# A selected LSTM step by step: the output gate multiplied after the choice of the weight set is known

## The reference

```python
x = x + gnn(layernorm(x))              # 10 rounds of graph propagation, 1250 nodes, 512 channels
x = x + lstm(layernorm(x)[None])[0]    # batch 1, 1250 steps, H = 512, S = 4 weight sets

def step(carry, x_t):
    h, c = carry
    sel_in = jnp.concatenate([h, c, x_t], axis=-1)
    logits = sel_in @ W_sel.T + b_sel
    onehot = jax.nn.one_hot(jnp.argmax(logits, axis=-1), Sx, dtype=x_t.dtype)
    g_all = einsum('bi,sgi->bsg', x_t, W_ih) + einsum('bh,sgh->bsg', h, W_hh) + b_ih + b_hh
    g = jnp.einsum('bsg,bs->bg', g_all, onehot)
    h2, c2 = _lstm_activate(g, c)      # i, f, g, o; c2 = s(f) c + s(i) tanh(g); h2 = s(o) tanh(c2)
    return ((h2, c2), h2)
```

## Time and profile before

| | us |
|---|---|
| median of the runs | 7712.02 |
| profiled execution | 7713.46 |
| its span | 7711.7 |
| loop A, 1484 to 2834 | 1350, 256 steps |
| loop B, 2842 to 7690 | 4848, 994 steps |
| PE busy | 6634.8 (86%) |
| DVE busy | 3545.5 (46%) |
| ACT busy | 1004.7 (13%) |

### The profile page before, as it was taken

One profiled execution on the slowest core, in us unless ns is written; L12 is line 12 of the kernel. 1 busy time (PEld: TensorE's weight loads), 2 busy tenths in 40 slices (PEclk: granted clock), 3 DMA queues, 4 the chain that ended last, 5 costly groups with the idle time before them and its releaser, 6 DMA issues. The chain is left out here.

```text
span 7711.7 us, 250693 instructions
## 1 busy us (share of the span) xinstructions
PE 6634.8 (86%) x85214; PEld 3513.4 (46%) x85215; DVE 3545.5 (46%) x16895; ACT 1004.7 (13%) x4031; POOL 945.3 (12%) x2829
## 2 busy tenths in 40 slices
PE   3467998899999998888888888888888888888888
PEld 3433444655555554444444444444444444444444
DVE  5523112355555554444444444444444444444444
ACT  0011001311111111111111111111111111111111
POOL 5703112200000000000000000000000000000000
PEclk6588998999999999999999999999999999999999
DMA  3220001622222210000000000000000000000000
GB/s 83 0 68 0 0 0 40 224 78 81 80 84 77 83 56 8 4 8 4 8 8 4 8 4 8 6 7 8 4 8 7 6 8 4 8 4 8 8 4 24
DMA packets 292938, 220.00 MB, mean 29 GB/s; under 512 B 137196, under 2 KB 268652, under 8 KB 290609
## 3 DMA queue, kind: packets, MB, share of 16 engines
q1 hardware_dynamic: 162612, 160.58, 6.2%
q10 hardware_dynamic: 106110, 59.01, 3.0%
q0 software_dynamic: 24192, 0.10, 1.0%
HBM read 160.28 MB, written 59.36 MB: 28 GB/s over the span
## 5 line engine op out<-in xcount | busy, mean ns | idle before, releaser
L1021 PE MATMUL ps<-WH,hparts 128*17 128x512 f16 x49760 | 2969.1, 380 | 148.9 <-DVE hparts L864 63.7
L1021 PEld LDWEIGHTS ps<-WH,hparts 128*17 128x17 f16 x49760 | 1305.0, 91 | 1316.2 <-DVE hparts L864 242.7
L840 DVE STREAM_TRANSPOSE gateT<-ps 128x512 f32<-128x512 f32 x1250 | 896.0, 717 | 2097.2 <-PE ps L1057 2088.0
L1091 PE MATMUL ps<-WH 128*128 128x512 f16 x4970 | 1246.1, 381 | 0.0
L467 POOL COPY xT<-hfull 128x4 f32 x1250 | 239.9, 192 | 5386.9 <-DVE hparts L862 5386.9
L1008 PE MATMUL ps<-wselT,acts 128*1 128x4 f32 x10000 | 430.5, 166 | 407.1 <-DVE acts L852 407.1
L972 PE MATMUL ps<-O,Adj 128*128 128x512 f16 x3000 | 650.3, 380 | 77.2 <-DVEq L749 77.2
L1091 PEld LDWEIGHTS ps<-WH 128*128 128x128 f16 x4970 | 404.6, 97 | 630.8 <-issue 278.7
L581 ACT ACTIVATE gateT<-gblk 128x16 f32 x1250 | 289.3, 231 | 2660.9 <-DVE pick L835 2618.4
L585 ACT ACTIVATE acts<-gates 128x16 f32<-128x16 f32 x1250 | 269.8, 216 | 2239.8 <-DVE gates L844 2239.8
L1065 PE MATMUL ps<-xT,wih_next 128*128 x2048 | 501.1, 388 | 65.1 <-DMA wih_next<-in_w_ih 34.0
(11 more groups left out here) (141 smaller groups left out, 4547.4 us busy)
## 6 DMA issues: line engine op xcount, KB each, us to landing
wih_next<-in_w_ih SPq DMA_DIRECT2D x256, 256.0 KB, 2.9
gblk<-gate_inputs ACTq DMA_DIRECT2D x48, 800.0 KB, 5.0
gate_inputs<-gx_next SPq DMA_DIRECT2D x64, 500.0 KB, 2.6
wst<-in_w_hh ACTq DMA_DIRECT2D x32, 512.0 KB, 7.6
wih<-in_w_ih SPq DMA_DIRECT2D x16, 1024.0 KB, 8.6
adjacency<-Adj SPq DMA_DIRECT2D x2, 6400.5 KB, 24.7
Adj<-adjacency SPq DMA_DIRECT2D x2, 6400.0 KB, 26.8
gate_inputs<-gstage SPq DMA_DIRECT2D x16, 500.0 KB, 6.0
```

What stands on the lines that cost most here:

```text
L840: dve.transpose(gateT[:, :, 0:32], gate_ps.rearrange("p (c q) -> p c q", q=32)).then_inc(turned, 1)
L1021: nc.tensor.matmul(gate_ps[32 * j:32 * j + 17, :], hparts[:, k, :], WH[:, s * KC + k, part, j, :], start=(k == 0 and part == 0), stop=(k = ...
L1091: nc.tensor.matmul(ps[:, 2, :], WH[:, 0, 0, 0, 0:P], WH[:, 0, 0, 0, :], start=True, stop=True)
```

## The change

Four things change, all in `cell` on DVE, in `act_block` on ACT, and in the step of PE.

1. The product is split. The cell part (input, forget and candidate gates) is multiplied with the guess, the output gate's part only once the pick is known. The input and forget gates take one matmul of 256 columns, the candidate one of 128 columns that goes into the forget gate's columns of PSUM, with the stationary operand shifted by one column, so that its sums land in rows 1 and 17 instead of 0 and 16. `gate_ps` shrinks to 256 columns. The output gate has a bank of its own, `ogate_ps`, 128 columns.
2. The seal goes. DVE now waits for `guess_mm` (four increments, one from the last matmul of each column group) and `settled` (either four at once from the sequencer of PE, when the guess was right, or one from each group's last matmul of the repeated cell part).
3. The output gate has its own chain: a transposing reduction out of PSUM, an addition of the input's share, and a tanh of its own on ACT. `osig` and `owsel` wait for that tanh.
4. PE's sequencer branches on the guess first. All else of a step, the logits too, stands within each of the four branches, and so does the comparison with the pick. The next guess is loaded behind the products and ahead of the pick. The weights of the selector are no longer scaled by 2^-13, and `owsel` is made from the tanh in one operation.

```diff
-                dve.wait_ge(gates_mm, n)
+                dve.wait_ge(guess_mm, n4)
+                dve.wait_ge(settled, n4)
                 dve.transpose(gateT[:, :, 0:32], gate_ps.rearrange("p (c q) -> p c q", q=32)).then_inc(turned, 1)
...
-                dve.tensor_reduce(gates[:, :], gateT[:, :, 0:33:16], AX.X, ALU.add).then_inc(gates_ready, 1)
+                dve.tensor_reduce(gates[:, :].rearrange("p (r b) -> p r b", r=2), turned_terms, AX.X, ALU.add).then_inc(gates_ready, 1)
+
+                dve.wait_ge(ogate_mm, n4)
+                dve.tensor_reduce(osum[:, 0, :], ogate_ps.rearrange("p (c q) -> p c q", q=32), AX.X, ALU.add,
+                                  apply_transpose=True).then_inc(oturned, 1)
+                dve.wait_ge(gates_ready, n)
+                dve.wait_ge(oturned, n)
+                dve.tensor_tensor(osum[:, 1, :], osum[:, 0, :], gates[:, 2 * SUB:3 * SUB], ALU.add).then_inc(osum_ready, 1)
...
-            def logits(t, n):
+            def logits(n):
...
-                pe.wait_ge(c_ready, n)
+                pe.wait_ge(owsel_ready, n)
...
+            def cell_products(s, done):
+
                 for k in range(KC):
                     for part in range(2):
                         for j in range(4):
-                            nc.tensor.matmul(gate_ps[32 * j:32 * j + 17, :], hparts[:, k, :], WH[:, s * KC + k, part, j, :],
-                                             start=(k == 0 and part == 0), stop=(k == KC - 1 and part == 1),
-                                             tile_position=(0, 32 * j))
+                            nc.tensor.matmul(gate_ps[32 * j:32 * j + 18, :], hparts[:, k, 1:19], WH[:, s * KC + k, part, j, 0:2 * P],
+                                             start=(k == 0 and part == 0), stop=False, tile_position=(0, 32 * j))
+                        for j in range(4):
+                            last = nc.tensor.matmul(gate_ps[32 * j:32 * j + 18, P:2 * P], hparts[:, k, 0:18],
+                                                    WH[:, s * KC + k, part, j, 3 * P:4 * P],
+                                                    start=False, stop=(k == KC - 1 and part == 1), tile_position=(0, 32 * j))
+                            if k == KC - 1 and part == 1:
+                                last.then_inc(done, 1)
+
+            def output_products(s):
+                for k in range(KC):
+                    for part in range(2):
+                        for j in range(4):
+                            last = nc.tensor.matmul(ogate_ps[32 * j:32 * j + 18, :], hparts[:, k, 1:19],
+                                                    WH[:, s * KC + k, part, j, 2 * P:3 * P], ...)
+                            if k == KC - 1 and part == 1:
+                                last.then_inc(ogate_mm, 1)
...
             def step(t, n):
-                pe.reg_load(guess, pick_row[0:1, bass.ds(t, 1)])
-                logits(t, n)
-                products_of(guess, n, True)
-                pe.wait_ge(pick_ready, n)
-                pe.sem_inc(pick_seen, 1)
-                pe.reg_load(chosen, pick[0:1, 0:1])
+                pe.reg_mov(guess, guess_next)
+
+                def guessed(s):
+                    logits(n)
+                    pe.wait_ge(h_ready, n)
+                    cell_products(s, guess_mm)
+                    pe.reg_load(guess_next, pick_row[0:1, bass.ds(t + 1, 1)])
+                    pe.wait_ge(pick_ready, n)
+                    pe.sem_inc(pick_seen, 1)
+                    pe.reg_load(chosen, pick[0:1, 0:1])
+                    with pe.If_eq(chosen, S - s):
+                        pe.sem_inc(settled, 4)
+                        output_products(s)
+
+                def repeated(s):
+                    cell_products(s, settled)
+                    output_products(s)
+
+                of_set(guess, guessed)
                 with pe.If_ne(chosen, guess):
-                    products_of(chosen, n, False)
-
-                nc.tensor.matmul(seal_ps, hparts[:, 0, 0:1], hparts[:, 0, 0:1], start=True, stop=True).then_inc(gates_mm, 1)
+                    of_set(chosen, repeated)
```

More of the change, by code:

```diff
@@ L250, in gnn_then_selected_lstm @@
         pick_seen = sem("pick_seen")
-        gates_mm = sem("gates_mm")
+        guess_mm = sem("guess_mm")
+        settled = sem("settled")
+        ogate_mm = sem("ogate_mm")
+        oturned = sem("oturned")
+        osum_ready = sem("osum_ready")
+        otan_ready = sem("otan_ready")
         turned = sem("turned")
@@ L871, in step @@
                 n = dve.snap(t + 1)
-                cell(t, n, dve.snap(t * 2 + 2))
+                cell(t, n, dve.snap(t * 2 + 2), dve.snap(t * 4 + 4))
                 choose(dve.snap(t + 2), dve.snap(t + 3))
@@ L888, in _ @@
                 step(t)
-            cell(dve.snap(N - 1), N, 2 * N)
+            cell(dve.snap(N - 1), N, 2 * N, 4 * N)
             for t in range(RT):
@@ L1020, in products @@
                         for j in range(4):
-                            nc.tensor.matmul(gate_ps[32 * j:32 * j + 17, :], hparts[:, k, :], WH[:, s * KC + k, part, j, :],
-                                             start=(k == 0 and part == 0), stop=(k == KC - 1 and part == 1),
-                                             tile_position=(0, 32 * j))
-            def products_of(chosen, n, first):
-                with pe.If_lt(chosen, 3):
-                    with pe.If_lt(chosen, 2):
-                        products(3, n, first)
+                            nc.tensor.matmul(gate_ps[32 * j:32 * j + 18, :], hparts[:, k, 1:19], WH[:, s * KC + k, part, j, 0:2 * P],
+                                             start=(k == 0 and part == 0), stop=False, tile_position=(0, 32 * j))
@@ new lines, in cell_products @@
+                        for j in range(4):
[9 more added lines that the diff above has]
+                            last = nc.tensor.matmul(ogate_ps[32 * j:32 * j + 18, :], hparts[:, k, 1:19],
+                                                    WH[:, s * KC + k, part, j, 2 * P:3 * P],
+                                                    start=(k == 0 and part == 0), stop=(k == KC - 1 and part == 1),
+                                                    tile_position=(0, 32 * j))
+                            if k == KC - 1 and part == 1:
+                                last.then_inc(ogate_mm, 1)
@@ L1030, in products_of, with of_set @@
+            def of_set(value, work):
+                with pe.If_lt(value, 3):
+                    with pe.If_lt(value, 2):
+                        work(3)
                     with pe.Else():
-                        products(2, n, first)
+                        work(2)
                 with pe.Else():
-                    with pe.If_lt(chosen, 4):
-                        products(1, n, first)
+                    with pe.If_lt(value, 4):
+                        work(1)
                     with pe.Else():
-                        products(0, n, first)
+                        work(0)
```

43 lines of the change are left out of this document (24 added, 19 removed).

## The result

The changed kernel takes 12,088.05 us (12,084.08 to 12,092.08, 3 runs) against 7,712.02, a ratio of 1.5675 (95% interval 1.5639 to 1.5711). The forecast was 9,800 with a range of 7,550 to 10,900: the direction and the cause held, the size did not.

The account below looks back on a forecast made before the run. Loop B was taken as bound by one chain from products through transpose to h, loop A by PE. 7713.5 + 20 (loop B) + 25 (loop A) + 2,100 (code reload) = 9,859, given as 9,800 us, range 7,550 to 10,900.

Parts of the forecast that it names:

- The first and the last block displace each other, a step of loop A pays twice: PE's code in loop A: nine blocks don't fit, so code reloads every step; 2,100 us in all, chance 0.53.
- R2: Rival: loop B's code doesn't fit either, so its 994 steps pay 8.2 us too; 18,000 us, chance 0.06.
- R1: Rival: all code fits and the step decides; 7,760 us, from 7,450 to 8,150, chance 0.41.
- 1.9 + 4.3 + 2 = 8.2 us a step: Loop A's code: last block half hidden, jump back in full, neighbours displaced by fetching ahead; times 256, 2,100 us.
- Loop A's own step, +25 forecast: Loop A without reload: PE itself is the chain, +0.1 us a step, +25 us over the loop.
- +0.45 for output part and idle PE: Loop A's step: 0.45 us added on PE, against -0.3 for the shorter cell part and the branches.
- Loop B, +20 forecast: Loop B: 764 right guesses at -0.05 us and 230 wrong ones at +0.25 us, +20 us in all.
- Product to transpose: Loop B, right guess: the sequencer's verdict ends the wait, transpose about 1.9 us after the first product instead of 1.96.
- Transpose to `h`: Cell on DVE and ACT: shorter transpose, output gate's reduction ahead of `cprod`; -0.05 us, between -0.15 and +0.4.
- Wrong guess: Loop B: PE idles between bodies until verdict, branches and first push; transpose at 4.05 us instead of 3.69, net +0.25.
- Worth nothing: The seal's removal: cell sums are there at 1.6 us, the verdict ends the wait, so no gain.
- R1a: Rival, code fits and step is faster: verdict at 1.75, output part ready with other reduction; -0.18 us, 7,490 us, chance 0.20.

Follow-up runs that it names:

- the shortened kernel: Changed kernel with loop A's code 115 instructions shorter (logits once ahead of the branches) and unused matmuls setting both loops to seven blocks each: 8,333.66 us, ratio 1.0817.
- the shifted one: Changed kernel with ten unused matmuls (20 instructions) ahead of loop A, which then lies on eight blocks instead of nine: 9,226.52 us.
- with two steps: Old step for steps 0 to 299, new step with both sequencer and wait edits behind it, without the 24 unused matmuls, last loop on eight blocks: 10,673.03 us.
- the load-first run: Shortened kernel with the next guess loaded before the cell products are pushed instead of behind them: 7,864.40 us, ratio 1.0201 to the kernel before.
- The two kernels with dead code: Kernel before with 470 or 600 never-executed matmuls at the end of loop A's step, jumped over in every step: 7,690.22 and 7,690.70 us.

## Why the prediction was wrong

**The code, cause right.** "The first and the last block displace each other, a step of loop A pays twice" was likelier than its rivals, and shown: loop A reloads, and loop B does not, so R2 fell. R1 (the code fits) fell as well. The Trainium skill's size for PE, eight blocks of 256 ("Runtime: NRT & Kernel Launch", "Instruction fetch mechanics"), is what the runs bear out: seven and the one fetched ahead fit, while eight and the one ahead do not. Its window of two blocks is not borne out; seven blocks stayed in loop B.

**The code, price wrong. This is the step that failed.** The term 1.9 + 4.3 + 2 = 8.2 us a step was 14.6, worth 3,738 us instead of 2,100. It counted two missing blocks and a few fetched ahead, some 3 packets a step (the text itself said 500 to 1,000 in all). There were 1,655, 6.5 a step. What was wrong is how often PE's code is waited for; a single stop was even shorter than reckoned. In loop A the sequencer stood for over 0.6 us in 3.2 branches a step, 11.7 us in all, and 1.3 times between other instructions, 2.4 us: 4.4 stops of 3.2 us each, where the term had two of 4.3, one of them partly hidden, and 2 us more. In the shortened kernel's loop A there is one such stop. By the count above, more than two blocks a step are missing when they are entered, and each block entered drags in its neighbour, which makes seven or so. Blocks still on their way when they are wanted may make the other stops; no run shows that. A packet cost about the same in three kernels: (5396 - 1658) / 1655 = 2.26 us in the changed kernel, (2560 - 1658) / 408 = 2.21 in the shifted one, 3245 / 1505 = 2.16 with two steps. The upper bound I gave, three missing blocks in full, 12.9 us, was below the truth too. Part of the price is the clock, at 0.61 of full speed in loop A, where PE idles between the units: a unit takes 3.0 us there instead of 1.95. How large a part it is, no run tells.

**Loop A's own step, +25 forecast, +308 measured.** "+0.45 for output part and idle PE" took PE as the chain. It is the sequencer: the late verdict, then the push of 64 instructions and the branches ahead of the unit, none of it covered. The 308 us are those of the shortened kernel, whose loop A has its logits in the old place.

**Loop B, +20 forecast, some +320 measured.** By terms for a right guess: branches first 0.06 (0.07 forecast, right). Product to transpose 2.13 and not 1.9: the sequencer's first instruction behind the last push came 0.86 us after the first product instead of 0.75, and the chain from there took 1.3 instead of 1.13. That it is the sequencer that ends this wait was right, and the load-first run shows it. Transpose to `h` +0.12 instead of -0.05: the transpose itself fell by 0.27 as forecast, but the waits written in an order that makes the late one an instruction of its own gave back 0.10, and output sum, addition and their hand-overs the rest. The diff showed two of these waits swapped, and I read nothing in it. Wrong guess +0.70 instead of +0.25: the verdict came 0.23 later than worked out, and the cell took 0.17 more. The bounds given, -0.25 to +0.6 for a right guess, hold the measured +0.19; the value was taken from their low end.

**The seal.** "Worth nothing" holds for the changed kernel, where the verdict ends the wait. On its own, in the kernel before, taking the seal away costs 0.07 us for a right guess. From the last product's start to the transpose's it is 0.51 us instead of 0.44. The Trainium skill's rule on side-by-side increments ("TensorE: Matmul & The Clock Gate", "The cost: per-tile semaphore tail"), about 26 ns each, makes 3 x 26 = 0.08 us, an estimate of this size; no run varies the number of increments alone, so the cause is not shown. The prediction had left it out for want of a row.

**The gain forecast in R1a** (-0.18 a step, if the verdict comes at 1.75) exists, though not in the change as it stood: with the load first and the waits in order it is 0.41 us a step of loop B with a right guess, and it shows in the time (0.9632) once loop A keeps the old step.

## What to carry to other kernels

Before a change that copies code into every branch, count the loop's instructions in blocks of the code's packets and by their position: seven blocks ran here without a reload, eight cost 3 to 4 us a step and nine 14.6, and a few unused instructions ahead of the loop decide which. Where a sequencer decides something that other engines wait for, write what isn't needed for the decision before its long push, and look who is behind it: in a loop where the sequencer is late anyway, the same edit gives nothing. Of two waits write first the one that ends last.

## What was not expected of the hardware

Of two waits ahead of an operation the second written becomes an instruction of its own; where it ends last, DVE's next operation starts 0.11 us after its input instead of 0.04. The two kernels with dead code, one run each, were 16 us faster (7,690 against 7,706 in the same comparison) than the kernel before: loop A rose from 5.29 to 5.43 us a step (a branch and a jump more), and loop B, whose instructions are the same on other blocks, fell from 4.88 to 4.83, all of it between first product and transpose (2.01 to 1.97). Why the place matters there, where nothing is reloaded, no run tells.
